# Four tables of step orders, rewritten, in a fused attention and feed-forward kernel

## The reference: what is computed

```python
x = x + 0.5 * ffn(layernorm(x))
x = x + attn(layernorm(x), weight)      # 16 heads of 16 features, softmax over 512 keys, 4096x256 projection
x = x + 0.5 * ffn(layernorm(x))
```

```python
qkv = shift_token(x) @ wqkv              # 8 heads of 64
q, k = rotary_xpos(l2norm(q) * qs, l2norm(k) * ksc)
x = x + local_attention(q, k, v) @ wo    # windows of 128 tokens, each looks at itself and the one before
h = layernorm(shift_token(x)) * lg + lb
a, g = split(h @ w1 + b1)                # 682 features each
x = x + (a * gelu(g)) @ w2 + b2
```

## Time and profile before

| | |
|---|---|
| time of the profiled execution | 4038.21 us, the median of the three |
| its span in the trace | 4036.5 us |
| PE busy | 3747.2 us, 93% |
| DVE busy | 2570.1 us, 64% |
| ACT busy | 2228.0 us, 55% |
| POOL busy | 2185.1 us, 54% |
| chain that ended last | PE 76%, DVE 11%, issue 5%, POOL 3%, DMA 2% |

### The profile page before, as it was taken

One profiled execution on the slowest core, in us unless ns is written; L12 is line 12 of the kernel. 1 busy time (PEld: TensorE's weight loads), 2 busy tenths in 40 slices (PEclk: granted clock), 3 DMA queues, 4 the chain that ended last, 5 costly groups with the idle time before them and its releaser, 6 DMA issues.

```text
span 4036.5 us, 75699 instructions
## 1 busy us (share of the span) xinstructions
PE 3747.2 (93%) x23552; PEld 3077.4 (76%) x23552; DVE 2570.1 (64%) x7288; ACT 2228.0 (55%) x5232; POOL 2185.1 (54%) x2175
## 2 busy tenths in 40 slices
PE   4999999999999699999999999978999999999997
PEld 3777777777777588888888888866777777777776
DVE  5676677666776365565555655656676676766774
ACT  2655665566556355444444444535755665566554
POOL 3565555455555255655555555644565555555652
PEclk8999999999999899999999999998999999999998
DMA  4000001110110100000000000110000011100100
GB/s 140 16 30 26 18 20 52 45 35 23 34 36 18 45 27 22 1 17 8 11 17 2 17 17 1 38 41 16 19 29 26 18 40 49 37 31 23 34 31 24
DMA packets 119046, 114.54 MB, mean 28 GB/s; under 512 B 13180, under 2 KB 116232, under 8 KB 118792
## 3 DMA queue, kind: packets, MB, share of 16 engines
q1 hardware_dynamic: 118792, 111.44, 8.6%
HBM read 73.69 MB, written 29.36 MB: 26 GB/s over the span
## 4 chain that ended last, share of the span: by engine, by line
PE 76%; DVE 11%; issue 5%; POOL 3%; DMA 2%; ACT 1%; SPq 1%; DVEq 0%; POOLq 0%; ACTq 0%
PE psum L1248 19%; PE psum L1250 17%; PE psum L1249 17%; PE psum L1350 6%; PE psum L1360 5%; PE psum L1374 5%; PE psum L1462 3%; PE psum L1339 2%; DVE nrm L1024 2%; DVE nrm L1022 1%; POOL ge_lo L617 1%; PE psum L1442 1%; DMA nrm<-xmid 1%; PE psum L1392 1%; DVE ssq L943 1%
## 5 line engine op out<-in xcount | busy, mean ns | idle before, releaser
L617 POOL TENSOR_TENSOR ge_lo<-ge,ge_hi 128x512 fp32r<-128x512 f32 x512 | 722.6, 1414 | 528.0 <-DVE ge_hi L1137 277.6
L580 POOL TENSOR_SCALAR probs<-probs,rz 128x256 f32<-128x256 f32 (+1 forms) x1024 | 444.6, 454 | 515.1 <-DVE rz L984 515.1
L801 ACT ACTIVATE ge<-psum 128x512 f32<-128x512 f32 x512 | 306.5, 599 | 611.6 <-PE psum L1462 611.6
L713 ACT ACTIVATE probs<-probs,nb,rq 128x256 f32<-128x256 f32 (+1 forms) x1024 | 575.9, 566 | 34.4 <-DVE nb L978 33.6
L1137 DVE CAST ge_hi<-ge 128x512 fp32r<-128x512 f32 x512 | 249.3, 488 | 531.0 <-ACT ge L801 526.6
L970 DVE CUSTOM_DVE_ANT_0 probs<-psum,mask 128x256 f32<-128x256 f32 (+1 forms) x1024 | 339.1, 387 | 283.1 <-PE psum L1350 283.1
L570 POOL TENSOR_TENSOR rinv<-ssq,minus_half 128x16 f32<-128x16 f32 x128 | 377.1, 2946 | 164.9 <-DVE ssq L947 161.0
L1248 PE MATMUL psum<-wqkv_hi,hT_hi 128*128 128x512 f32 x768 | 334.9, 436 | 59.4 <-DVE turned_sin L936 56.4
L694 ACT ACTIVATE squares<-psum 128x512 f32<-128x512 f32 x256 | 150.0, 599 | 372.6 <-PE psum L1250 245.2
L590 POOL TENSOR_TENSOR hid_lo<-gate,hid_hi 128x512 fp32r<-128x512 f32 x160 | 205.2, 1282 | 252.6 <-ACT hid_hi L744 252.6
L1250 PE MATMUL psum<-wqkv_lo,hT_hi 128*128 128x512 f32 x768 | 307.2, 400 | 0.0
(11 more groups left out here) (163 smaller groups left out, 10575.9 us busy)
## 6 DMA issues: line engine op xcount, KB each, us to landing
xnext<-stream SPq DMA_DIRECT2D x32, 512.0 KB, 4.2
xmid<-stream SPq DMA_DIRECT2D x32, 512.0 KB, 3.9
stream<-xmid SPq DMA_DIRECT2D x16, 512.0 KB, 2.9
nrm<-xmid SPq DMA_DIRECT2D x32, 224.0 KB
wbuf<-L_ffn_wqkv SPq DMA_DIRECT2D x8, 768.0 KB, 7.7
wbuf<-L_ffn_w SPq DMA_DIRECT2D x8, 682.0 KB, 5.6
x_all<-L_attn_x SPq DMA_DIRECT2D x8, 512.0 KB, 7.7
stream<-x_all SPq DMA_DIRECT2D x8, 512.0 KB, 3.9
```

Of the source, the lines that this page charges most:

```text
L580: last = nc.gpsimd.tensor_scalar(pu, pu, rz[:, h, t:t + 1], 1.0, ALU.mult, ALU.mult)
L617: nc.gpsimd.tensor_tensor(ges[1][:, k % 4, :], ge[:, k % 4, :], f32(ges[0][:, k % 4, :]), ALU.subtract).then_inc(S["g_lo"], 1)
L713: last = nc.scalar.activation(pu, pu, ACT.Exp, bias=nb[:, h, t:t + 1], scale=rq[:, 0, t, h:h + 1], accum_out=zs[:, h, t:t + 1])
L801: nc.scalar.activation(ge[:, k % 4, :], RB[k % 2], ACT.Exp, scale=GSCALE, accum_out=gz[:, h, t:t + 1]).then_inc(S["g_exp"], 1)
```

## The change

The four tables are permuted. Each holds the same steps as before, each step the same instructions; SP's order is the same. The last steps of PE's table show the kind of change (`-` before, `+` after):

```diff
 PE_STEPS, from W2 on
-W2 W3 B +K1 +k3 +Q1 +q3 +Q2 +v0 +v1 +v2 n0 n1 +v3 +Q3 g0 a0 +K2 g1 a1 +K3 g2
+W2 W3 B +Q1 +v1 +v2 +K1 +q3 +k3 +K2 n0 n1 +v3 +Q2 g0 a0 g1 +Q3 a1 +K3 g2
 PE_STEPS, from S2 to S6
-S2 -g4 T0 S3 -w1 T1 S4 -a4 -w2 T2 A0 S5 A1 T3 S6
+S2 T0 -a3 +z0 -g4 +z1 -a4 S3 T1 A0 S4 A1 T2 S5 -w2 S6
```

More of the change, by code:

```diff
@@ L34 @@
 SHIFTED = P - 16
[L41 to L59, removed]
+PE_STEPS = ("S0 -g3 -w0 S1 -w1 -a2 S2 T0 -a3 +z0 -g4 +z1 -a4 S3 T1 A0 S4 A1 T2 S5 -w2 S6 T3 -w3 A2 S7 T4 A3 +q0 "
+            "T5 +k0 -g5 +k1 A4 T6 -w4 +q1 +Q0 A5 A6 -w5 T7 +k2 +q2 W0 A7 +K0 W1 +v0 W2 W3 B +Q1 +v1 +v2 +K1 +q3 "
+            "+k3 +K2 n0 n1 +v3 +Q2 g0 a0 g1 +Q3 a1 +K3 g2").split()
+ACT_STEPS = ("-G2 -G3 E0 E1 i0 -u2 H0 E2 i2 +zh0 +zh1 -G4 -u3 H1 E3 i1 O0 H2 E4 E5 H3 E6 -u4 H4 O1 E7 +sq0 H5 +sk0 "
+            "-G5 +sk1 H6 -u5 +sq1 +Qc0 H7 +sk2 +sq2 O2 f0 O3 f1 +Kc0 +vh0 +Qc1 +vh1 +vh2 +sq3 +Kc1 +sk3 +Kc2 nh0 "
+            "nh1 +vh3 G0 f2 +Qc2 G1 +Qc3 u0 +Kc3 u1").split()
+DVE_STEPS = ("X0 X1 R0 -y2 X2 i0 R1 -y3 L0 +zl0 +zl1 -y4 R2 X3 i2 L1 X4 i1 R3 X5 L2 R4 P0 X6 L3 R5 X7 L4 P1 R6 "
+             "+rq0 L5 +ss0 R7 +rk0 -y5 L6 +rq1 +c0 +rk1 +ss1 -F -e L7 +ss2 +rq2 +rk2 P2 f0 P3 f1 +c1 +c2 x l r "
+             "+rq3 j +ss3 nl0 nl1 B +rk3 y0 f2 +c3 y1 +Y").split()
+POOL_STEPS = ("-ul1 N0 -ul2 N1 N2 N3 -ul3 N4 N5 N6 +b0 -ul4 +p0 +d0 -ul5 N7 +b1 +p1 +d1 +p2 +d2 +b2 s +b3 +p3 +d3 "
+            "ul0").split()
 def steps(table, n, prev, nxt, only=None):
```

## The result

The changed kernel takes 4246.66 us (median of 4 runs, 4243.48 to 4248.1), the kernel before beside it 4036.67 us. The ratio is 1.0513, with a 95% interval of 1.0492 to 1.0534: 210 us slower, where +115 was forecast. The profiled execution took 4246.81 us, its span is 4245.1 us.

The account below looks back on a forecast made before the run. PE bounds the kernel, so a permutation can win only its waits. The terms 7 + 56 + 42 + 10 = 115 on 4038.2 give 4153 us; range 4115 to 4190, 8 in 10 for 4085 to 4215.

Parts of the forecast that it names:

- T7's margin: At T7, with N7 now behind p0, d0 and ul5: 0.2 us of room, so no cost.
- Parts 1 and 2: W3 to n0: less PE cover, shorter chain from x; n0's wait 4.2 against 3.9 us, +7 in all.
- Part 3: New PE waits among the scores, at S3, S4, S6 and T0: 2.0 us a round, +56 in all.
- Part 4: Clock falls to half behind n0's single wait: 1.4 us a round, bounds 0 and 2.5, +42 in all.
- a rival's mechanism: Thin margins at w5, T7 and W2 break: 1.0 to 2.5 us a round, 4180 to 4225 us; chance 0.16.
- The other two margins (w5, W2): Room of 0.5 us at w5 and 0.3 at W2, costing nothing while it holds.
- Part 5: Four rounds that load weights, at W3, P2 about 3 us nearer to it: 2.5 us each, +10 in all.

Follow-up runs that it names:

- experiment 1: The kernel after, with 28 transposes of the identity put into PE's wait ahead of n0: 4177.59 us, ratio 1.0342.
- Experiment 5: The kernel before, with one exchange on POOL, p3 ahead of d3: 4009.17 us, ratio 0.9931.
- Experiment 6: The kernel after, with v0 back behind W3 on PE: 4235.87 us, ratio 1.0497.
- Experiments 7: The kernel after, with POOL's N7 and ul5 moved ahead of d0: 4300.48 us, ratio 1.0655.
- 8: The kernel after, with the turns z0 and z1 and their readers zh, zl moved back behind A3: 4289.35 us, ratio 1.0633.
- Experiments 10: The kernel before, with p3 ahead of d3 on POOL and the weight casts f0, f1 behind O3 on ACT and P3 on DVE: 3998.21 us, ratio 0.9902.
- 11: The kernel after, with the weight casts f0, f1 behind O3 on ACT and P3 on DVE: 4229.68 us, ratio 1.0469.
- 9: The kernel before, with p3 ahead of d3 and b3 ahead of s on POOL, and r behind rq3 on DVE: 4012.18 us, ratio 0.9942.
- 12: The kernel before, with p3 ahead of d3, casts f0, f1 behind O3 and P3, and DVE's F ahead of L5: 3990.67 us, ratio 0.9883.
- experiments 2: The kernel after, with 16 transposes of the identity put into PE's wait ahead of n0: 4200.35 us, ratio 1.0405.
- 4: The kernel after's tables up to W2, the kernel before's from there on, on all four engines: 4207.53 us, ratio 1.0413.
- experiment 3: The kernel before's tables until W2, the kernel after's from there on, on all four engines: 4223.3 us, ratio 1.0461.

## Why the prediction was too small

The direction was right and each of the five parts happened; what failed is the size of terms, and the sum was short by 95 us. Two were put at nothing: T7's margin (0.6 us a round measured) and the 48 bias products of a load round (14.5 us in all). The low clock was put at 42 us, where experiment 1 measures 69. By its own steps, for one ordinary round (6.22 us longer):

| step | predicted | measured |
|---|---|---|
| Parts 1 and 2, from K1 or Q1 to n0 | +0.25 | +0.6 (loss of 4.5, before 3.9) |
| Part 3, waits among the scores | +2.0 | 1.8 idle, 2.6 from start to start |
| margin at T7 | 0 | +0.6 |
| Part 4, clock | +1.4 | +2.5 |
| sum | +3.65 | +6.3 |

This is a round with the long stretch of low clock. The mean over the 26 ordinary rounds is 5.5 longer, of which 1.9 is the clock (experiment 1) and 3.6 waits, against 1.4 and 2.25 forecast.

**Parts 1 and 2: right in kind, 0.35 too small.** x to n0 was forecast at 10.9 and is 11.1, with one long instruction in j where there had been two. Experiment 5 shows it alone, 0.98 a round. The loss of cover is as given: n0 now waits 4.4 idle, forecast 4.2. Experiment 6 shows that this cover can't be had back for nothing, since v0 also covers P2.

**Part 3: the places right, 0.6 too small, read from the trace only.** Waits of L1350 for the maximum at S4 and S6, one for `hT_lo` at S3, T0 a little late. What I did not see is A1 (0.25). Experiments 7 and 8 were meant to price these waits one by one and did not: taking one away made larger ones. That the waits cost their length in the round is therefore argued from PE being without a break elsewhere, and not shown by a run.

**The margin of T7: a rival's mechanism, as an addition.** I gave T7 0.2 us of room, and it waits 0.60. POOL around it:

```profile
558.29 2.91 POOL L570 TENSOR_TENSOR rinv<-ssq,minus_half 128x16 f32<-128x16 f32 x1
561.17 1.29 POOL L565 TENSOR_TENSOR turned_qk<-turned_qk,turned_sin 128x512 f32<-128x512 f32 x1
562.41 1.28 POOL L590 TENSOR_TENSOR hid_lo<-hid_r,hid_hi 128x512 fp32r<-128x512 f32 x1
563.68 2.30 POOL L580 TENSOR_SCALAR probs<-probs,rz 128x256 f32<-128x256 f32 x4
```

POOL runs without a break through p0, d0, ul5 and N7, so N7's end is set by the sum of what stands ahead of it. The rival had 1.0 to 2.5 for such a break; this one costs 0.6. The other two margins (w5, W2) held.

**Part 4: a mis-sized term.** I took the length of the low stretch from one row of the kernel before, 3.4 us, and let part of it fall into the wait: 1.4 a round, 42 in all. Experiment 1 measures 69 in all by taking it away. In the kernel after the clock fell to 0.50 at each of the 26 steady n0, for 6.8 us at 13 of them and for 3.4 at the other 13. A long stretch costs 2.5 (experiment 1) or 2.6 (experiment 6), a short one about 1.3, so 2.5, which I had as the bound, is what about half of the rounds lose. The row that I used was true but ended too early: right behind it the clock fell again.

```profile
790.50:797.30 6.80, 6.80 (x31) 5.90 (x31) 2.19 (x9) 1.19 (x2) 2.91 (x1) 0.50 0.53 141
```

And behind the wait of 9.9 at the last round's n0 it was low for 13.7 us in all. The trace before had three lengths, and I treated one as a constant.
The Trainium skill ("TensorE: Matmul & The Clock Gate", "HAM oscillation — how this bites in real kernels") tells of a matmul kernel whose clock falls again in every turn of its loop, behind the wait for data. The trace agrees: here it fell to 0.50 at every steady n0.

**Part 5: far too small, as it left out a term.** I gave 10 us for the rounds that load weights. The stretches that hold them or their neighbours grew by 67 us (12.4 + 12.4 + 19.6 + 22.6). They hold six rounds, of which each would have grown by the 3.65 forecast, 22 in all; so 45 stands against my 10. The 10 was meant for W3's wait, and for that it was right in total: the four load rounds of the kernel before wait 0, 4.9, 0 and 2.95 us there (I took all four to be like the second), those of the kernel after 2.35, 6.9, 2.4 and 6.9, 10.7 more. What I put at nothing is the 48 bias products behind W3. Before they took 4.8, 5.8, 4.8 and 5.8 us, after 8.9 in all four, wholly at the low clock: 14.5 more. The load round of the first call shows where. PE in it: first W3 behind its wait and the 48 bias products of the kernel after, then these products in the kernel before, and in a load round of the kernel before with the clock at 1.00 throughout them.

```profile
847.25 0.58 PE L1248 MATMUL psum<-wo_hi,oT_hi 128*128 128x256 f32 x1 [6.90 <-DVE oT_lo L992]
...
849.98 8.92 PE L1306 MATMUL psum<-lnp,wbuf 128*128 128x1 f32 x48
```

```profile
786.39 5.82 PE L1306 MATMUL psum<-lnp,wbuf 128*128 128x1 f32 x48
...
136.69 4.78 PE L1306 MATMUL psum<-lnp,wbuf 128*128 128x1 f32 x48
```

ACT of the kernel after, at f0, which waits for the weights' DMA:

```profile
843.18 1.62 ACT L641 ACTIVATE w_hi<-wbuf,lnp 128x1280 fp32r<-128x1280 f32 x2 [7.99 <-DMA wbuf<-L_ffn_w]
```

P3 stands behind f0 on DVE, and f0 waits for a DMA of the weights. From f0's start on ACT to W3 there are 4.1 us in both kernels, but PE now comes to W3 earlier, so W3 waits 6.9 instead of 4.9. The low clock that follows lies over all of the bias products. These are on the chain between x and n0, which is 20.4 us long there instead of 16.8: SP issues the shift only 1.4 us behind their end in both kernels (860.30 and 793.60). Experiments 10 and 11 take W3's wait away and win 11 and 17 us; in the latter PE then waits 3.4 at the bias products, which still take 9.1 at the low clock in two of the four rounds. So the order of f0 and P3 is shown to be part of it. What is left of the 45 beyond the 25 of W3 and the bias products was not taken apart by a run.

**The count.** Experiment 1 splits the growth of the span (208.6, forecast 115, so 94 short) in two. The low clock, as far as it goes away there, is 66.5 of it, 24 more than the 42 forecast. For the rest, experiment 1 against the kernel before: the ordinary rounds are 3.61 longer than before, against 2.25 forecast, 35 in all over 26; the stretches with the load rounds grew by 49, against 23.5 (six times 2.25, and 10), so 26 more; and Parts 1 to 3 were summed over 28 and 30 rounds, while the sum of intervals has all 32 of them, 9 more. The end of the kernel gives 1 back. So the largest piece is not the clock but the waits of ordinary rounds, and among them T7, to which I had given nothing (0.6 a round, some 16 in all).

**Late rounds of the second call.** Five rounds there last 85.8 to 88.6, up to 3.4 more than the typical one. DVE shows idle time at X0 that no semaphore explains (and 1.63 us more two us later):

```profile
3886.46 0.29 DVE L970 CUSTOM_DVE_ANT_0 probs<-psum,mask 128x128 f32<-128x128 f32 x1 [3.38 <-issue]
```

In the whole execution this happens 11 times, 24.3 us in all, and not in the kernel before. It comes with more traffic of the instruction queue (155 packets, 1.26 MB, before 129 and 1.06). PE waits 1.6 to 2.0 us for it at a score step in each such round, some 9 of the 35 above. It is not the low clock: experiment 1 has the same idle time (23.6 us in 11 times) with the clock at 1.00. It is there in all nine runs with PE's order of the kernel after or a half of it, and in none of the four experiments that keep PE's order of the kernel before (5, 9, 10 and 12). That fetching of instructions is the cause is a guess; no run tested it, and it stays open.

## What to carry to other kernels

When an order is changed on the engine that sets the time, count its idle time per round and also how it is divided: four short waits of 3.3 us in all left the clock alone here, one of 4.4 us cost another 1.9 as a mean. Where work that covers a chain is taken away, the chain must get shorter by as much, so shorten the chain first: one exchange on POOL won some 29 us by itself, and lost among the four rewritten tables it could not be seen. And treat waits in a table of steps as a system: of four attempts to take one wait out of the slower order, two cost 54 and 43 us and two won 11 and 17.

## What the runs showed of the hardware

**The clock against the length of one idle piece of PE.** Counted at the 26 steady n0 of each run. With one piece of 1.7 to 2.0 us before n0 the clock fell once (experiment 9). With 2.1 to 2.9 it fell 13 times (experiment 2) or 21 times (experiment 4, where the piece stands at v1), with 3.3 (once 4.4) 24 times (experiment 6), with 4.0 to 4.7 each time, for 3.4 or 6.8 us (the kernel after), and with 6.8 to 7.7 each time, for 6.8 or 10.2 us (experiment 3). In experiments 2 and 4 pieces of the same length came with a fall and without one, so the length alone does not decide. 28 small transposes of an identity in the idle time held it at 1.00, with 0.8 to 1.6 us left idle.

**The price of a low stretch depends on what follows.** In the kernel after one of 3.4 us costs about 1.3. In experiment 4 PE works through all of one, but n0's wait of 1.1 behind it goes, and the round is under 1 us longer.

**Small operations of DVE are blocked too.** An operation of 128x4 with two inputs takes 0.17 us as a rule and this much while POOL subtracts a 128x512 tile (second row):

```profile
1231.65 1.02 DVE L978 TENSOR_TENSOR nb<-mx,rq 128x4 f32<-128x4 f32 x1
```

```profile
1231.36 1.29 POOL L590 TENSOR_TENSOR hid_lo<-gate,hid_hi 128x512 fp32r<-128x512 f32 x1 [1.16 <-ACT hid_hi L744]
```

It stands on the way from the scores to the exponential, so what follows it on DVE comes some 0.85 us later. The Trainium skill ("SBUF — State Buffer", "SBUF: two separate sides") describes the lock between the two engines for an operation with two inputs, held for the whole instruction. The trace agrees: in the kernel after 54 of these small operations begin while POOL is in such a subtraction, and each ends only with it (0.40 to 1.04 us instead of 0.17). Being small does not spare them.

**Many tiny products at the low clock.** 48 products of one column took 4.78 us with the clock at 1.00 throughout, 5.82 with 2.4 us of it low, and 8.92 wholly at 0.50, about 100 ns each against 186: such work is slowed nearly twofold by the clock as well, though each product has only one column.
